# Experts' weights split inside the second cross attention, and the experts' last norm on ScalarE

## The reference, cut to what matters

```python
x = _layernorm(x + _L1_xattn_ref(x, ctx_1024, ctx_1024, Wq, Wk, Wv, Wo), axis=-1)
x = _layernorm(x + _L1_ffn_ref(x, router_w, e_bias, Wg, Wu, Wd, SWg, SWu, SWd), axis=-1)
# _L1_ffn_ref
coef = jnp.zeros((T, E)).at[jnp.arange(T)[:, None], topk_idx].add(topk_w)
g = jnp.einsum('th,ehi->tei', x, Wg)
u = jnp.einsum('th,ehi->tei', x, Wu)
h = jax.nn.silu(g) * u * coef[:, :, None]
moe_out = jnp.einsum('tei,eih->th', h, Wd)
shared = jax.nn.silu(x @ SWg) * (x @ SWu) @ SWd
```

## Time and profile before

| | us |
|---|---|
| median of 3 runs | 4009.61 (4009.27 to 4018.98) |
| the profiled execution's own time | 4014.4 |
| its span in the profile | 4012.6 |
| TensorE busy | 3414.4 (85%) |
| VectorE busy | 3038.1 (76%) |
| ScalarE busy | 2356.9 (59%) |
| GpSimd busy | 1842.3 (46%) |

### The profile page before, as it was taken

The page is one execution under the profiler, slowest core; times in us unless marked ns, Lnnn a source line. Parts: engine busy times, 40 slices in busy tenths (PEclk is TensorE's granted clock), DMA queues, the critical chain, the costliest instruction groups (busy, mean ns, idle before and its releaser), DMA issues. The chain is left out here.

```text
span 4012.6 us, 91730 instructions
## 1 busy us (share of the span) xinstructions
PE 3414.4 (85%) x30917; PEld 2194.5 (55%) x30917; DVE 3038.1 (76%) x6227; ACT 2356.9 (59%) x5257; POOL 1842.3 (46%) x2322
## 2 busy tenths in 40 slices
PE   6899999998665882899999968888399999999998
PEld 3466666665444872566666657777244444444443
DVE  6777777776674662899999948888588888888887
ACT  1355555654763442799899946565355555555555
POOL 1000000000553663677777722222187777778776
PEclk9999999999887775899999978898699999999999
DMA  2000000000112212000000012222376565556663
GB/s 82 6 11 9 10 9 10 10 9 25 43 51 64 67 49 41 17 18 20 18 18 18 12 46 57 55 58 54 110 160 139 128 136 126 131 126 138 132 136 85
DMA packets 279473, 243.93 MB, mean 61 GB/s; under 512 B 57832, under 2 KB 205324, under 8 KB 279308
## 3 DMA queue, kind: packets, MB, share of 16 engines
q1 hardware_dynamic: 267916, 237.21, 24.9%
q10 hardware_dynamic: 11392, 4.79, 0.5%
HBM read 210.34 MB, written 31.59 MB: 60 GB/s over the span
## 5 line engine op out<-in xcount | busy, mean ns | idle before, releaser
L2650 POOL TENSOR_TENSOR d_hidden<-d_gated,d_upper 128x512 f32<-128x512 f32 x528 | 802.2, 1544 | 259.8 <-DVE d_upper L2759 131.7
L2766 DVE TENSOR_TENSOR d_h_low<-d_hidden,d_h_high 128x512 f16<-128x512 f32 x528 | 540.8, 1024 | 118.1 <-ACT d_h_high L2726 116.8
L2720 ACT ACTIVATE d_gated<-d_g 128x512 f32<-128x512 f32 x528 | 315.2, 597 | 493.2 <-PE d_u L2666 493.2
L750 POOL MEMSET f_minus_half<- 128x4 f32 x1 | 0.1, 101 | 864.4 <-POOLq L37 864.4
L2759 DVE TENSOR_TENSOR d_upper<-d_u,d_coef 128x512 f32<-128x512 f32 x512 | 349.2, 682 | 61.4 <-issue 28.2
L2726 ACT ACTIVATE d_h_high<-d_hidden 128x512 f16<-128x512 f32 x528 | 328.4, 622 | 8.2 <-POOL d_hidden L2650 8.2
L1825 ACT ACTIVATE c_sc<-c_sc,c_negmax 128x129 f32<-128x129 f32 x1024 | 326.3, 394 | 9.0 <-issue 4.0
L2664 PE MATMUL d_g<-d_x_high,w_Wg_high 128*128 128x512 f16 x528 | 201.8, 382 | 92.4 <-DVE d_upper L2759 56.1
L1653 POOL TENSOR_TENSOR c_posg<-w_pos,c_gate 128x512 f32<-128x512 f32 x256 | 265.9, 1039 | 0.0
L1732 PE MATMUL c_turned<-all_ident,c_sc 128*128 128x128 f32 x1024 | 180.6, 302 | 35.4 <-ACT c_sc L1825 34.6
L2664 PE MATMUL d_o<-d_h_high,w_Wd_high 128*128 128x512 f16 x528 | 201.4, 381 | 2.0 <-ACT d_h_high L2726 1.6
(11 more groups left out here) (408 smaller groups left out, 9649.8 us busy)
## 6 DMA issues: line engine op xcount, KB each, us to landing
d_coef<-coefT SPq DMA_DIRECT2D x256, 512.0 KB, 7.2
d_cT<-in_ctxT SPq DMA_DIRECT2D x128, 64.0 KB, 2.0
mx_x<-in_xT SPq DMA_DIRECT2D x16, 256.0 KB
b_x<-in_x SPq DMA_DIRECT2D x64, 64.0 KB
y<-b_y SPq DMA_DIRECT2D x64, 64.0 KB, 1.6
f_y<-y SPq DMA_DIRECT2D x16, 256.0 KB, 3.9
f_x<-in_x SPq DMA_DIRECT2D x16, 256.0 KB, 3.7
x<-f_res SPq DMA_DIRECT2D x16, 256.0 KB, 2.4
```

The costliest lines, as they stand in the source:

```text
L2650: nc.gpsimd.tensor_tensor(hidden[b][:], gated[b][:], upper[b][:], ALU.mult).then_inc(h_ready, 1)
L2720: nc.scalar.activation(gated[b][:], ps_g[i][:], ACT.Silu, scale=1.0 / W_SCALE).then_inc(silu_ready, 1)
L2766: nc.vector.tensor_tensor(h_low[b][:], hidden[b][:], h_high[b][:], ALU.subtract).then_inc(h_low_ready, 1)
```

## The change

The nine pieces of `setup_moe` are gone. The host lays the three matrices into one array of 99 units. In column 0 of the cross attention three units are taken, and in each of the 48 looped columns two: SyncE loads 128 KB into a buffer of its own (one of four, by the column's place in the turn) ahead of the column's other loads, ScalarE scales it in place and copies it to f16 at the end of its column, and GpSimd takes the remainder at the end of its own. The load waits until the remainder of the load before it is done. The f16 tiles are allocated around both phases.

In the experts, `norm` becomes four ScalarE instructions, one in each of the units 12 to 15, on a multiplier and an offset. VectorE's `add` keeps only the sum in unit 6; `stats` stand in units 7 and 8, two tiles each, and `gather` in unit 9, with one more small instruction (`minus_mean`). `power` moves to unit 10 and has one more small instruction (`offset`); the preparation of the next group's x moves from unit 16 to 17. The wait for the store before last moves from `norm` to `add`.

```diff
+                def load_units(it, j):
+                    chunk, n, _, part = units(it, j)
+                    if not isinstance(it, int):
+                        sp.wait_ge(w_low_ready, n - 1)
+                        sp.sem_inc(sp_waited, 1)
+                    sp.dma_start(stage[j][:, part, :], experts_w[:, chunk, :]).then_inc(w_loaded[j], 16)
...
                     if coefs is not None:
                         sp.dma_start(coefT[:, coefs_tile], coefT_sb[cs][:]).then_inc(coef_stored[cs], 16)
+                    if units(it, j):
+                        load_units(it, j)
                     run(load_x, beside(it, j, 4))
...
+                def low_parts(it, j):
+                    chunk, n, _, part = units(it, j)
+                    pool.wait_ge(w_high_ready, n)
+                    nc.gpsimd.tensor_tensor(experts[1][:, chunk, :], stage[j][:, part, :], experts[0][:, chunk, :], ALU.subtract).then_inc(w_low_ready, 1)
...
                     run(power, beside(it, j, -1))
+                    if units(it, j):
+                        low_parts(it, j)
...
+                def high_parts(it, j):
+                    chunk, n, times, part = units(it, j)
+                    act.wait_ge(w_loaded[j], 16 * times)
+                    nc.scalar.activation(stage[j][:, part, :], stage[j][:, part, :], ACT.Copy, scale=W_SCALE).then_inc(w_scaled, 1)
+                    act.wait_ge(w_scaled, n)
+                    nc.scalar.activation(experts[0][:, chunk, :], stage[j][:, part, :], ACT.Copy).then_inc(w_high_ready, 1)
...
                     run(copy_e, beside(it, j, 0), 1)
+                    if units(it, j):
+                        high_parts(it, j)
...
-    PREP, COPY_OUT, TURN, ADD, POWER, NORM = 16, 4, 5, 6, 7, 9
+    PREP, COPY_OUT, TURN, ADD, POWER, NORM = 17, 4, 5, 6, 10, 12
...
                     nc.gpsimd.tensor_tensor(rstd[s][:], var_eps[s][:], minus_half[:], ALU.pow).then_inc(rstd_ready, 1)
+                    pool.wait_ge(rstd_ready, nth(it, j))
+                    nc.gpsimd.tensor_tensor(offset[s][:], minus_mean[s][:], rstd[s][:], ALU.mult).then_inc(offset_ready, 1)
...
+                def norm(it, j, q):
+                    s = j % U
+                    if q == 0:
+                        act.wait_ge(offset_ready, nth(it, j))
+                    last = nc.scalar.activation(res[s][:, q, :], y[s][:, q, :], ACT.Identity, bias=offset[s][:, q:q + 1], scale=rstd[s][:, q:q + 1])
...
-                def norm(it, j):
-                    s = j % U
-                    dve.wait_ge(rstd_ready, nth(it, j))
-                    dve.wait_ge(stored[s], 16 * (it + 1) if j >= 0 else 16 * it)
-                    for q in range(QT):
-                        last = nc.vector.tensor_scalar(res[s][:, q, :], y[s][:, q, :], mv[s][:, q, 0:1], rstd[s][:, q:q + 1], ALU.subtract, ALU.mult)
-                    last.then_inc(y_ready, 1)
...
-                        if u == NORM and previous is not None:
-                            norm(*previous)
+                        if u == ADD + 1 and previous is not None:
+                            stats(*previous, (0, 1))
+                        if u == ADD + 2 and previous is not None:
+                            stats(*previous, (2, 3))
+                        if u == ADD + 3 and previous is not None:
+                            gather(*previous)
...
-        with Phase(nc, "w4") as ph:
-            w = setup_cross1(nc, ph, inputs("cross1"), ident)
-            phase_cross1(nc, w, x4, d["ctxT"], x5, x5T, coefT)
         with Phase(nc, "w5") as ph:
-            w = setup_moe(nc, ph, inputs("moe"), ident)
-            phase_moe(nc, w, x5, x5T, coefT, out)
+            parts, weights = expert_weights(ph)
+            with Phase(nc, "w4") as ph:
+                w = setup_cross1(nc, ph, inputs("cross1"), ident)
+                phase_cross1(nc, w, x4, d["ctxT"], x5, x5T, coefT, parts, d["moe_W"])
+            phase_moe(nc, dict(weights, ident=ident), x5, x5T, coefT, out)
```

More of the change, by code:

```diff
@@ L1990, in setup_cross1, with phase_cross1 @@
     return w
-def phase_cross1(nc, w, x4, ctxT, x5, x5T, coefT):
+def phase_cross1(nc, w, x4, ctxT, x5, x5T, coefT, experts, experts_w):
     U, HD, PAIRS, N, E, G = 4, D // H, H // 2, 4, 64, 8
@@ L2024, in phase_cross1 @@
         etop, total, minus_half = ph.sb("etop", [P, N, 8]), ph.sb("total", [P, N]), ph.sb("minus_half", [P, 1])
+        stage = [ph.sb(f"stage{j}", [P, AT_ONCE if j == 0 else 2, P]) for j in range(U)]
+        w_loaded = [ph.sem(f"w_loaded{j}") for j in range(U)]
         scored = ph.ps("scored", [P, 4, 512])
@@ L2039, in phase_cross1 @@
          bn_ready, mv_ready, var_ready, rstd_ready, offset_ready, x5_ready, logits_exp, rates_ready, score_ready, router_own,
-         coef_ready, waited, pool_waited, sp_waited) = (ph.sem(n) for n in names)
+         coef_ready, waited, pool_waited, sp_waited, w_scaled, w_high_ready, w_low_ready) = (ph.sem(n) for n in names)
         def nth(it, j):
@@ L2075, in pipelined @@
                 column(0, j)
-            with eng.Fori(3, steps - 1) as it:
+            with eng.Fori(LOOP_FROM, steps - 1) as it:
                 for j in range(U):
@@ L2080, in pipelined, with units @@
                 column(steps - 1, j)
+        def units(it, j):
+            if not isinstance(it, int):
+                return bass.ds(2 * U * it + (2 * (j - U * LOOP_FROM) + AT_ONCE), 2), U * it + (j - U * LOOP_FROM + 2), it + (1 - LOOP_FROM + (j == 0)), slice(0, 2)
+            return (slice(0, AT_ONCE), 1, 1, slice(0, AT_ONCE)) if U * it + j == 0 else None
         def run(part, position, *more):
@@ L2463, with expert_weights @@
 W_SCALE, H_SCALE = 256.0, 16.0
[L2466 to L2498, removed]
+def expert_weights(ph):
+    parts = [ph.sb(f"W_{part}", [P, 3 * UNITS, P], F16) for part in ("high", "low")]
+    return parts, {k: [part[:, n * UNITS:(n + 1) * UNITS, :] for part in parts] for n, k in enumerate(("Wg", "Wu", "Wd"))}
 def phase_moe(nc, w, x5, x5T, coefT, out):
@@ L2530, in phase_moe @@
         var_eps, rstd = slots("var_eps", [P, QT]), slots("rstd", [P, QT])
+        minus_mean, offset = slots("minus_mean", [P, QT]), slots("offset", [P, QT])
         minus_half = ph.sb("minus_half", [P, QT])
@@ L2742, in group @@
                             copy_out(*previous)
+                        if NORM <= u < NORM + QT and previous is not None:
+                            norm(*previous, u - NORM)
                 def drain(it, j):
@@ L2747, in drain @@
                     copy_out(it, j)
+                    for q in range(QT):
+                        norm(it, j, q)
                 looped(nc.scalar, lambda: high_x(0, 0), group, drain)
@@ L2808, in drain @@
                     add(it, j)
-                    norm(it, j)
+                    stats(it, j, range(QT))
+                    gather(it, j)
                 for j in range(U):
```

28 lines of the change are left out of this document (20 added, 8 removed).

## The result

The changed kernel took 3918.32 us (median of 4 runs, 3914.62 to 3925.71), the kernel before 4009.44 in the same comparison: a ratio of 0.9777, 95% interval 0.9758 to 0.9796. The sign and the mechanisms were right, the size was not: -91 us in place of -55.

A forecast was written before the change was run, and what follows sets the result against it. TensorE was taken to bound the experts, TensorE and VectorE level in the cross attention. -28.4 + 2 - 34.4 + 4.5 + 1.2 = -55.1 us from 4014.4 profiled, less 4.8 for the median, gave 3955 us, range 3940 to 3984.

The forecast's parts named there:

- The weights' phase, -28.4: Before the experts: the stretch from the first weight load to the x5T load goes, -28.4 us.
- The cross attention, +2: Cross attention's loop: the weights' scaling, copy and remainder in 48 columns are nearly hidden, +2 us.
- the cover that I had read from one column: Cross attention: ScalarE's added 0.8 us a column fits into its 1.52 us wait for the offset before `norm`.
- the ring of load and split: Cross attention: load, split and next load limit the column if landing exceeds 4.3 us; rival slower than before, 4073 us, chance 0.03.
- the 45 I gave: Cross attention's loop: ScalarE's wait for the offset falls from 83.5 to about 45 us.
- The boundaries, -34.4 + 4.5: Experts' 15 group boundaries: stalls behind `add` (1.25 us) and `norm` (1.04) go, -34.4; some waiting stays, +4.5.
- the 0.3 us left over: Experts: TensorE time still lost at each group boundary after the change, 4.5 us in all.
- The five loop turns I leave as they are: Experts' loop: five TensorE waits of about 4.1 us where the loop turns stay unchanged, 0 us.
- a rival of 0.09: More than forecast: loop turns shrink with VectorE's shorter list or columns meet better, up to 15 us more, 3940; chance 0.09.
- The end, +1.2: End of the experts: nothing hides the last norm on ScalarE, the product and the small instruction, +1.2 us.

The follow-up runs named there:

- the experiment at twice the price: Changed kernel with two more ScalarE instructions on the weights in each of 48 columns: 3943.99 us; with 100 idle ScalarE semaphore increments added ahead of the experts: 3917.02 us.
- the weights alone: Kernel before with only the weights' load and split moved into the cross attention, the experts' phase as before: 3955.13 us, ratio 0.9853.
- the norm alone: Kernel before with only the experts' new norm, statistics and power, the weights' own phase kept: 3940.94 us, ratio 0.9824.
- the changed kernel with 40: Changed kernel with 40 semaphore increments that nobody waits for, on VectorE ahead of the experts' loop: 3947.84 us, ratio 0.9832.
- everything in unit 6: Changed kernel with VectorE's statistics, aggregates, small instruction and epsilon behind the sum in unit 6 again, norm still on ScalarE: 3936.65 us, ratio 0.9807.

## Why the prediction was wrong

**The weights' phase, -28.4: right.** Measured -28.1.

**The cross attention, +2: right, nearly free.** +0.7, and the experiment at twice the price shows the cover that I had read from one column. VectorE was not blocked either: busy 314.6 us of the 380, against 316.0 before. The load of 128 KB lands in 2.1 us (estimate 2.5), so the ring of load and split never tightened. ScalarE's two instructions take 0.42 each (0.41), GpSimd's remainder 0.67 (0.6). The wait for the offset fell from 83.5 to 59.9, not to the 45 I gave, for the cover has a second part that I had not seen, the wait for `d_edge` in `empty_edge`. It was this in the kernel before, and is 7.6 now:

```profile
ACT d_raw L2277 <- PE d_edge L2250: 25.4, 27, 1.4
```

**The boundaries, -34.4 + 4.5: right in mechanism, both sizes off.** The 2.29 us of stalls went altogether; the 0.3 us left over, 4.5 in all, did not come. And 30 stalls cost 0.17 each beyond their bracket, 5.1 us, which I left out by adding up brackets. -29.9 was forecast, 15 x 2.61 = -39.2 came.

**"The five loop turns I leave as they are": the failed step.** They were worth 30.4 us and I put them at 0, with 15 us as the far end of a rival of 0.09. I had the row, 5.91 us "issue", and took it for a constant of the loop. It was an accident of place that any edit ahead of the loop on VectorE could end. My rival had the turns shrink with the shorter list, and that isn't the mechanism either: the weights alone keep 312 instructions and have no stall. I also priced it by TensorE's wait of 4.1. A turn cost 140.4 - 134.3 = 6.1: the wait, its 0.17, and the low clock behind it, in the kernel before:

```profile
3164.00:3169.00 5.00, 1.33 (x7) 0.39 (x4) 0.20 (x1) 1.11 (x2) 0.03 (x1) 0.92 0.37 98
3169.00:3174.00 5.00, 4.36 (x11) 1.59 (x12) 3.83 (x6) 1.11 (x2) 3.71 (x3) 0.50 0.01 2
```

In the second stretch TensorE does 11 matmuls where some 23 fit at 0.215 us each.

**The start: not foreseen, +6.** What is left of the -63.6 when 39.2 and 5 x 6.1 = 30.4 are taken out is +6.0. Two rows show it directly. The first group, which has no boundary and no turn before it, takes 72.2 us from its first gate to the next group's, against 66.0 in the kernel before. And the norm alone, with the weights' phase between and the same turns of 129.1, has first to last gate 1031.8 against 1038.7. The experts now begin right behind the cross attention, and in all eight kernels with that order and no delay at the start VectorE waits 2.7 to 7.3 us for the second chunk of coefficients, against 0 to 1.3 in the four with the weights' phase between. The stall's own length, its overlap and the low clock behind it make the sum. Why the chunk is late is open: holding the fourth back changes nothing, and neither the third alone nor the nearness of the router's stores was tried.

**The end, +1.2:** +0.7, for the product took 0.20 and the small instruction 0.17.

The sum, with what was measured: -28.1 + 0.7 - 39.2 - 30.4 + 6.0 + 0.7 = -90.3, and 1.6 for the phases before is -88.7, the difference of the spans.

## What to carry to other kernels

An engine that stands at a loop's turn for "issue" is not paying a constant: look at where its looped list lies, for every engine, and expect any edit ahead of the loop to move it, also in kernels built only to test something else. Price a stall of TensorE from start to start of its matmuls, not by the bracket, and add the clock that it costs when it is some microseconds long. And where two parts of a change are each measured alone, compare their sum with both together, for what is counted twice is a mechanism that belongs to neither.

## What the runs showed of the hardware

**Where a looped list may lie.** Over fourteen kernels the stall is there or not by the list's place alone. A place is the number of an instruction in its engine's list, counted in the program as built:

| engine | stall | no stall |
|---|---|---|
| VectorE | 3067-3379, 3083-3395, 3088-3394 | 3048-3354, 3051-3363, 3052-3364, 3063-3369, 3139-3451 |
| ScalarE | 2047-2398 | 2026-2367, 2029-2370, 2030-2381, 2033-2384, 2147-2498 |

The stall is 4 to 6 us a turn with about five more packets of 8 KB. The trace has each packet's time, and counting VectorE's instructions gives its place then. In the kernel before, one turn's packets start at 3302.4, 3307.7, 3310.4, 3328.3 and 3389.0, with VectorE at place 3375, at the list's first instructions (two packets), at 3120 and at about 3250. In the changed kernel with 40, whose list begins 21 places later, they start at place 3374, at the list's first instructions (two), and at about places 3128 and 3252. So the borders stay where they are when the list moves, near 3118, 3246 and 3374, and one packet is a piece of about 128 instructions. Each list that stalls touches four such pieces, and each that doesn't touches three and fetches nothing at its turns. For ScalarE a border lies between 2385 and 2398, and the others 128 apart from it.

The Trainium skill (page "Runtime: NRT & Kernel Launch", section "Instruction fetch mechanics") says that most engines keep two blocks of 256 instructions, and that a taken branch to a block outside of them forces a fetch before execution goes on. The branch agrees: VectorE stands behind the turn, and a packet starts there. The block of 256 doesn't agree with the packets, which start every 128 places or so. The places alone fit both readings, two blocks of 256 or three pieces of 128, and no kernel here lies where the two differ. By the pieces of 128, an estimate: a list of 306 to 312 instructions touches only three in about six of ten places, one of 351 in about one of four.

**The clock behind a stall.** After TensorE stood for 3.42 or 4.31 us, its granted clock was 0.50 (1.2 GHz) for about 5 us; after 1.25 and 1.04 us its matmuls kept their 0.38.

**A small VectorE instruction beside GpSimd.** The 128x4 one took 0.83 us beside GpSimd's product and ended with it, the same relation as in the earlier trace rows, here on one input. With everything in unit 6, where no product of GpSimd runs beside it, all sixteen took 0.17. The changed kernel, then that one (ns, min/median/max):

```profile
L2816 DVE TENSOR_SCALAR d_minus_mean<-d_mv x16: 170/830/835, 2962.0 to 3916.8; 128x4 f32<-128x4 f32 x16
```

```profile
L2816 DVE TENSOR_SCALAR d_minus_mean<-d_mv x16: 170/170/171, 2956.8 to 3936.5; 128x4 f32<-128x4 f32 x16
```
